# First sweep over the adjacency matrix in panels of 1024 rows with units of 256 columns, and a new assignment of its SBUF slots

## What is computed

```
d   = rsqrt(sum(adj, axis=1) + 1e-6)
L0  = (d[:,None] * (adj + I) * d[None,:]) @ (x @ w)
x1  = layernorm(x + L0)
agg = adj @ x1
msg = relu(agg @ W_msg.T + b_msg)
out = layernorm(x1 + gru_cell(msg, x1))
```

## Time and profile before

| | |
|---|---|
| median of 3 runs | 2015.1 us |
| the profiled execution | 2017.33 us, span 2015.3 us |
| granted TensorE clock, mean | 0.938 |
| PE busy | 1770.9 us (88%) |
| DVE busy | 1380.9 us (69%) |
| ACT busy | 640.4 us (32%) |
| HBM read | 545.79 MB, 273 GB/s over the span |

### The profile page before, as it was taken

How to read it: one execution, slowest core, us unless ns; L and a number is a source line. 1 busy time by engine, 2 the same in 40 slices (tenths; PEclk the granted TensorE clock), 3 DMA queues, 4 the chain that set the end, 5 groups by cost and what they waited for, 6 DMA issues and landing times.

```text
span 2015.3 us, 17025 instructions
## 1 busy us (share of the span) xinstructions
PE 1770.9 (88%) x6500; PEld 1200.8 (60%) x6500; DVE 1380.9 (69%) x1189; ACT 640.4 (32%) x561; POOL 130.5 (6%) x118
## 2 busy tenths in 40 slices
PE   0245777888888999999999999999999999999996
PEld 0123333434444444447888888888777777777774
DVE  6777776755576556558766666556678787878785
ACT  0000000000000000014444444444466565656563
POOL 0000000000000000012000000000000111011101
PEclk9767788888888999999999999999999999999998
DMA  9999999977789878755666666566799898989892
GB/s 356 387 373 353 339 341 335 335 250 251 255 311 320 298 260 300 273 190 189 199 194 200 200 201 195 189 197 192 260 358 311 289 323 296 316 287 326 294 318 78
DMA packets 284480, 551.12 MB, mean 273 GB/s; under 512 B 17648, under 2 KB 18160, under 8 KB 284400
## 3 DMA queue, kind: packets, MB, share of 16 engines
q1 hardware_dynamic: 280832, 541.13, 77.9%
q0 software_dynamic: 2560, 8.39, 1.2%
q10 hardware_dynamic: 1008, 0.53, 0.1%
HBM read 545.79 MB, written 4.19 MB: 273 GB/s over the span
## 4 chain that ended last, share of the span: by engine, by line
PE 76%; DMA 13%; SPq 6%; DVE 4%; issue 1%; ACT 1%; POOL 0%; DVEq 0%; ACTq 0%
PE bank L305 20%; PE bank L339 16%; PE bank L341 15%; PE bank L340 15%; DMA kept<-adj_blocks 8%; SPq L242 5%; DMA ring<-adj_blocks 3%; DVE colsum L591 3%; PE bank L292 2%; DMA spare<-adj_blocks 1%; DVE csum L595 1%; PE bank L404 1%; PE bank L417 1%; PE bank L415 1%; PE bank L410 1%
## 5 line engine op out<-in xcount | busy, mean ns | idle before, releaser
L601 DVE TENSOR_TENSOR lo<-ring,hi 128x2048 fp32r<-128x2048 f32 x204 | 465.4, 2288 | 265.4 <-ACT f L492 198.0
L486 ACT ACTIVATE hi<-ring 128x2048 fp32r<-128x2048 f32 x204 | 391.1, 1917 | 381.0 <-DMA ring<-adj_blocks 228.2
L339 PE MATMUL bank<-hi,x1s 128*128 128x512 f32 x1024 | 417.1, 407 | 6.1 <-DVE x1s L651 4.1
L341 PE MATMUL bank<-hi,x1s 128*128 128x512 f32 x1024 | 400.1, 391 | 0.0
L340 PE MATMUL bank<-lo,x1s 128*128 128x512 f32 x816 | 318.7, 391 | 0.0
L305 PE MATMUL bank<-kept,feat 128*128 128x512 f32 x608 | 294.9, 641 | 13.3 <-DMA kept<-adj_blocks 13.3
L591 DVE TENSOR_TENSOR colsum<-colsum,ring 128x2048 f32<-128x2048 f32 x106 | 243.0, 2293 | 77.8 <-DMA ring<-adj_blocks 77.8
L591 DVE TENSOR_TENSOR colsum<-colsum,kept 128x2048 f32<-128x2048 f32 x97 | 222.4, 2293 | 82.0 <-DMA kept<-adj_blocks 82.0
L305 PE MATMUL bank<-ring,feat 128*128 128x512 f32 x528 | 247.6, 625 | 18.6 <-DMA ring<-adj_blocks 18.6
L339 PEld LDWEIGHTS bank<-hi,x1s 128*128 128x128 f32 x1024 | 192.9, 188 | 56.2 <-issue 7.2
L465 ACT ACTIVATE dege<-bank 128x4 f32<-128x4 f32 x16 | 2.8, 174 | 685.1 <-PE bank L292 685.1
(11 more groups left out here) (87 smaller groups left out, 1394.7 us busy)
## 6 DMA issues: line engine op xcount, KB each, us to landing
ring<-adj_blocks SPq DMA_DIRECT2D x656, 512.0 KB, 6.1
kept<-adj_blocks SPq DMA_DIRECT2D x202, 512.0 KB, 8.4
more<-adj_blocks SPq DMA_DIRECT2D x104, 512.0 KB, 6.0
spare<-adj_blocks SPq DMA_DIRECT2D x62, 512.0 KB, 10.2
xt<-x_t SPq DMA_DIRECT2D x16, 256.0 KB, 8.1
xin<-x POOLq DMA_DIRECT2D x16, 256.0 KB, 3.5
out<-y POOLq DMA_DIRECT2D x16, 256.0 KB, 6.1
wih_s<-wih_t ACTq DMA_DIRECT2D x1, 192.0 KB, 6.5
```

Source lines behind the costliest of these rows:

```text
L339: pe.matmul(acc[:, :], fh, ah, start=start and c == 0, stop=False, skip_group_check=True)
L341: mm = pe.matmul(acc[:, :], fl, ah, start=False, stop=stop and c == KC - 1, skip_group_check=True)
L486: ins = act.activation(hi[:, n % NHI], raw(slot_of2[n]), ACT.Copy)
L601: ins = dve.tensor_tensor(flat(low(n)), flat(raw(slot_of2[n])), flat(hi[:, n % NHI]).bitcast(f32), ALU.subtract)
```

## The change

The first sweep goes by 8 panels of 1024 rows, each of 32 **units** of 256 columns: [128, 2, 1024], again 1 MB and the same work for DVE (one addition of 128x2048) and PE (2 column blocks x 2 halves of the rows, 4 matmuls of 128x512). A unit is one whole block of HBM, fetched by one DMA with runs of 8 KB. The number of panel ends goes from 16 to 8.

Early are all units left of the diagonal block, the 4 on it, and for panels 0 to 2 the 4 of the block right of it: 39 blocks of 1024 x 1024, or 156 tiles. N2 becomes 100. A burst has 8 units in panels 1 to 3 and 4 in the others.

There are 17 slots in panels 0 to 3 and 15 after; each unit gets the slot whose release the planner estimates to come first. The last 8 units take slots 4 to 11 only. The last three low units (LATE), not two, come behind the degrees. `xt` has one buffer of 1024 rows, and `load_xt(P+1)`, at the 17th unit of panel P, waits for `support(P)`, which PE runs behind the burst of panel P-1.

The second and third stages load as before, by tiles with runs of 2 KB; `split_hi` waits for the slots 12 to 14 that `hi` overlays.

```
-    def kept_tile(i, k):
-        return i <= k <= i + 2 and k - i <= depth(k)
-    RING1 = [0, 1, 2, 3, 10, 11, 12]
-    KEEP = [4, 5, 6, 7, 8, 9]
+    NP, NU, WP = N // 1024, 32, 1024
+    BAND = (0, 1, 2)
+    LATE = 3
+    def kept_unit(P, j):
+        return j // 4 == P or (P in BAND and j // 4 == P + 1)
+    def early_unit(P, j):
+        return j // 4 < P or kept_unit(P, j)
     def early(i, k):
-        return k < i or kept_tile(i, k)
+        return early_unit(i // 2, 2 * k)
     def panel_order(P):
+        low = list(range(4 * P))
+        far = [j for j in range(4 * P, NU) if not kept_unit(P, j)]
+        kept = [j for j in range(4 * P, NU) if kept_unit(P, j)]
+        head, tail = low[:max(0, 4 * P - LATE)], low[max(0, 4 * P - LATE):]
+        mixed = sorted([((q + 0.5) / len(head), 0, j) for q, j in enumerate(head)] +
+                       [((q + 0.5) / len(far), 1, j) for q, j in enumerate(far)])
+        body = [j for _, _, j in mixed]
+        cut = min(len(body), 20)
         return body[:cut] + kept + body[cut:] + tail
...
+    burst = {P: ([(P - 1, j) for j in range(4 * P, 4 * P + 4)] if P - 1 in BAND else []) +
+                [(P, j) for j in range(4 * P, 4 * P + 4)] for P in range(NP)}
...
+    come, pe_at = 0.0, 0.0
+    for P in range(NP):
+        for j in panel_order(P):
+            n = len(slot_of1)
+            slots = range(4, 12) if n >= NP * NU - 8 else range(17 if P < 4 else 15)
+            s = min(slots, key=lambda s: free[s])
...
+            come = max(come + 1, free[s] + 2.5)
+            if j < 4 * P:
+                pe_at = max(pe_at, come + (8 if j in after_degrees[P] else 0)) + 1.4
+                free[s] = pe_at
+            else:
+                free[s] = 1e9 if kept_unit(P, j) else come + 1
+        pe_at = max(pe_at, come + 6)
+        for t in burst[P]:
+            pe_at += 1.4
+            free[slot_of1[at1[t]]] = pe_at
...
             def load_xt(P):
-                if P >= 2:
-                    sp.wait_ge(supp_done, P - 1)
-                sp.dma_start(xt[:, P % 2, :], x_t[:, P * W:(P + 1) * W]).then_inc(xt_in[P % 2], 16)
+                if P:
+                    sp.wait_ge(supp_done, P)
+                sp.dma_start(xt[:, :], x_t[:, P * WP:(P + 1) * WP]).then_inc(xt_in, 16)
...
+            for n, (P, j) in enumerate(T1):
                 if before1[n] is not None:
                     slot_free1(before1[n])
                 s = slot_of1[n]
-                load(s, P, k)
+                sp.dma_start(unit(s), adj_blocks[P * NP + (P - j // 4) % NP, j % 4]).then_inc(slot_in[s], 16)
+                if n == 2:
                     load_xt(0)
+                if n % NU == 16 and P + 1 < NP:
                     load_xt(P + 1)
...
+            def product(P, j):
+                n = at1[(P, j)]
+                first = first_product[P] == (P, j) and P > 0
+                if first and P >= 2:
+                    pe.wait_ge(evicted, 2 * P - 2)
+                pe.wait_ge(slot_in[slot_of1[n]], loads1[n] * 16)
+                for u in range(2):
+                    for h in range(2):
+                        mm = pe.matmul(bank[P % 2 * 2 + h][:, :], feat0[:, j * 2 + u, :],
+                                       unit(slot_of1[n])[:, u, h * W:(h + 1) * W], start=first and u == 0,
+                                       stop=final_product[P] == (P, j) and u == 1, skip_group_check=True)
                 mm.then_inc(prod_done, 1)
...
+            for P in range(NP):
+                for j in before_degrees[P]:
+                    product(P, j)
                 degrees(P)
+                for j in after_degrees[P]:
+                    product(P, j)
+                pe.wait_ge(feat0_ready, P + 1)
+                for Q, j in burst[P]:
+                    if (Q, j) == (P, 4 * P):
+                        add_self(P)
+                    product(Q, j)
+                if P + 1 < NP:
                     support(P + 1)
...
             split_hi(0)
             split_hi(1)
+            evict(NP - 1)
             split_hi(2)
```

More of the change, by code:

```diff
@@ new lines, in gnn_resnorm_kernel @@
+    products = []
+    for P in range(NP):
+        products += [(P, j) for j in before_degrees[P] + after_degrees[P]] + burst[P]
+    product_no = {t: n + 1 for n, t in enumerate(products)}
+    first_product = {P: min((t for t in products if t[0] == P), key=lambda t: product_no[t]) for P in range(NP)}
+    final_product = {P: max((t for t in products if t[0] == P), key=lambda t: product_no[t]) for P in range(NP)}
+    free = {s: 0.0 for s in range(17)}
+    held, count = {}, {s: 0 for s in range(17)}
@@ L114, in gnn_resnorm_kernel @@
             first = (N2 % 4)
-            order = [(first + j) % 4 for j in range(4)] + [13, 14]
+            order = [(first + j) % 4 for j in range(4)] + [17, 18]
             s = order[(n - N2) % 6]
@@ L200, in raw, with unit @@
                 return kept[:, s - 4]
-            return spare[:, 0] if s == 12 else more[:, s - 13]
+            if s < 15:
+                return pool3[:, s - 12]
+            return spare[:, s - 15] if s < 17 else more[:, s - 17]
+        def raw(s):
+            return slot(s).rearrange("p (c r) -> p c r", c=KC)
+        def unit(s):
+            return slot(s).rearrange("p (u r) -> p u r", u=2)
         def low(n):
             s = slot_of2[n]
-            return lo[:, s] if s < 4 else more_lo[:, s - 13]
-        slot_in = [sem(f"slot_in{s}") for s in range(15)]
-        xt_in = [sem(f"xt_in{s}") for s in range(2)]
+            return lo[:, s] if s < 4 else more_lo[:, s - 17]
+        slot_in = [sem(f"slot_in{s}") for s in range(19)]
+        xt_in = sem("xt_in")
         xin_in = [sem(f"xin_in{s}") for s in range(2)]
@@ L289, in degrees @@
                     pe.wait_ge(deg_ready, P)
[L290 to L293, removed]
+                for b in range(WP // 128):
+                    mm = pe.matmul(p_deg[:, b:b + 1], csum[:, b * 128:(b + 1) * 128], ones[:, :], start=True, stop=True)
                 mm.then_inc(deg_done, 1)
[L296 to L307, removed]
-                mm.then_inc(prod_done, 1)
@@ L316, in add_self @@
             def add_self(P):
-                for c in range(KC):
-                    pe.matmul(bank[P % NACC][:, c * 128:(c + 1) * 128], feat0[:, P * KC + c, :], ident[:, :],
-                              start=P == 0 and c == 0, stop=False, skip_group_check=True)
+                for c in range(WP // 128):
+                    pe.matmul(bank[P % 2 * 2 + c // KC][:, c % KC * 128:(c % KC + 1) * 128],
+                              feat0[:, P * WP // 128 + c, :], ident[:, :],
+                              start=P == 0 and c % KC == 0, stop=False, skip_group_check=True)
@@ L754, in _ @@
             pool.wait_ge(zeroed, 4)
-            for P in range(NT):
+            for P in range(NP):
+                t0 = P * WP // 128
                 pool.wait_ge(deg_ready, P + 1)
-                pool.tensor_tensor(dinv[:, P * KC:(P + 1) * KC], dege[:, :], mhalf[:, :], ALU.pow)\
-                    .then_inc(dinv_ready, 1)
+                pool.tensor_tensor(dinv[:, t0:t0 + WP // 128], dege[:, :], mhalf[:, :], ALU.pow).then_inc(dinv_ready, 1)
             def load_rows(q):
```

176 lines of the change are left out of this document (72 added, 104 removed).

## The result

The changed kernel takes 1920.66 us (median of 4 runs, 1918.99 to 1921.81), the kernel before 2013.82 us (4 runs); the ratio is 0.9536, with a 95% interval of 0.9519 to 0.9552. The forecast was 1937 us, a gain of 80 us on the profiled span; that span went from 2015.3 to 1918.1 us, so the gain is 97.

A forecast was written before the change was run, and what follows sets the result against it. The prediction saw waits for slots and products leaving neither PE nor DMA full before 900 us. First sweep -98, seam +7.7, second stage +8.0, +1 and +1 gave -80 on 2017.3: 1937 us, range 1912 to 1988.

The forecast's parts named there:

- The price of a load: First-sweep loads: a 1 MB unit in 8 KB runs takes 2.55 us, ends 2.32 and 2.71.
- 105 units lie on the path (31 + 32 + 3 x 14): Panels 0 to 4: only these loads set the time, so 2.71 us each gives +17, 2.32 gives -24.
- PE's chain: Ends of panels 1 to 3: from the last unit's landing through degrees, low units and burst to `support`, 51.7 us.
- `load_xt` decides: Panels 2 to 4: SP's wait there for `support` sets the length, 95 us each where loads alone need 82.9.
- PE's panels: Panels 5 to 7, bound by PE: 87.6, 101.4 and 115.1 us from degrees to degrees.
- the 5 us that I added for low clock: Rest of the first sweep: PE's reduced clock adds 5 us, as in old panel 13; last product at 799.
- The seam: First sweep to second stage: T2[1] waits for a late slot; last product to `layer1(0)` 18.8 instead of 11.1 us, 7.7 lost.
- Given back in the second stage: Second stage: layer 0 of three more tiles costs 8.0 us, row 12 costs 1, a later GRU step 1.
- row 12: Second stage: its `x1` is needed at tile 7 but queued at tile 8 of DVE; 0 to 3 us, taken as 1.
- (a): Rival on first-sweep loads: 8 KB runs load no faster than 2 KB, 2.71 us a unit, 1954 us; chance 0.17.
- (b): Rival on slots: panels still wait for slots in turn, panels 5 and 6 take 120 us each, 1988 us; chance 0.15.
- (c): Rival on first-sweep loads: 8 KB runs lower the rate, 3.3 us a unit, slower than before at 2038 us; chance 0.06.

## Why the prediction came out as it did

**The price of a load.** Taken 2.55, measured 2.48 us. The term was mis-sized within its ends. Degrees of panel 4 came 11.2 us earlier than forecast. In panels 0 and 1 this is the price: together 3.7 us, for 63 loads x 0.07 = 4.4 (panel 0 alone is 1.3 late, as DVE starts late). Panels 2 to 4 were 7.4 us shorter in sum, where the 3 x 14 loads of my sum give 2.9; that all 160 loads x 0.07 make 11.2 is no proof, since another step was wrong there. Of the two figures in the Trainium skill (DMA: Bandwidth & Descriptors), the 425 GB/s of Bandwidth, Measured was nearly met (422). The same section says that about 358 GB/s is what each core gets when both cores of a pair stream. This program runs on one core, so the prediction was wrong to read the figure in Specifications as a bound for it.

**How many loads are on the path.** "105 units lie on the path (31 + 32 + 3 x 14)" is the step that failed. By it the 0.23 us between 2.71 and 2.48 are 24 us; the runs showed 46.6. I had let each of panels 2 to 4 start anew at the wait for `support`, with an empty queue and 5.9 us to the first unit. In the trace the queue isn't empty then; the hole lies 17 to 20 us long right behind a panel's end, where 15 of 17 slots are held, and the panel is 32 loads (79.4), 1.2 for `xt` and some 12 of hole and dip: 92. My sum of PE's chain was right (51.7 us to the end of `support`; measured from the last landing at 169.9 to 220.6, 50.7), but it isn't what the end of the panel hangs on; with 43 for what follows it gave 95 for another reason. I had both mechanisms in the text, and added up the wrong one. That 95 came near the measured 92 to 93 was luck; moving `load_xt` alone (-1.6 us) shows it.

**`load_xt` decides.** Wrong for this kernel, right for those with free slots: behind the first hole it is the next in line, at the same length. Two waits stood one behind the other, and either alone gives 91 to 93 us for panel 2.

**PE's panels.** Right to 0.3 us each, from one duration of 3.43 us per unit and 1.7 and 1.8 for the small steps. With the clock at 1.00 all through these panels, the 5 us that I added for low clock weren't there; they were taken from panel 13 before, where PE had idled.

**The seam.** Right to the tenth (18.8), and by its cause: the exchange of two slots took it away. The tenth is luck: with the same slots other executions show 18.9 to 21.8 us, as T2[1] lands sooner or later.

**Given back in the second stage.** +9.2 for 10 forecast. `layer1(7)` did not wait for row 12: no wait of PE for it stands in the trace.

**Rivals.** (a) is refuted as a fact (the rate did rise). Its time, 1954, was 13 us too early for the kernel with 2.71 us a load, by the count of loads above. (b) did not come true, because slots go by estimated release: with a fixed rotation the same panels are slower than the kernel before. The estimate has no `load_xt`, degrees or `support` in it and was good enough for panels 5 to 7. (c) did not occur.

So of the gain of 93 us 47 are the loads by one DMA with runs of 8 KB, measured with everything else in place. The other 46 are slots, panels and kept blocks together, net of the 8 us lost at the seam and the 9 behind it. How they part between fewer panel ends and more slots wasn't measured; with a fixed rotation the whole is a loss of 42.

## What to carry to other kernels

When two waits lie on one queue, the one that is longer in a table of waits need not be the one that costs: look for the stretch where the throughput of the resource falls, and name the wait that stands there. Change the price of a transfer in one run, and compare the response, panel by panel, with the number of transfers times the change: 15.3 us for 64 x 0.23 was the count itself, 11.4 us for 32 x 0.23 said that something else had grown with it. When another limit goes away, look at the granted clock of the engine that now waits: here that took back 3.3 us. In a planned assignment of buffers, look up what the first steps of the next stage inherit: one slot here cost 7.7 us, and an exchange of two numbers gave it back.

## What the runs showed of the hardware

Loads of 1 MB into 128 partitions from SP's queue, one core, run at 387, 409 and 422 GB/s with runs of 2, 4 and 8 KB (2.71, 2.56, 2.48 us per 1.05 MB), the first two in DMAs of 512 KB, the last in DMAs of 1 MB; whether 8 KB runs in smaller DMAs do as well wasn't tried. Beside such a stream the seven small loads of another queue at the start come later, the longer the runs: with 2, 4 and 8 KB the last was there at 12.2, 15.4 and 22.1 us. Idle time of PE shows in its clock: 68 matmuls took 18.96 us at granted clock 1.00 and 22.29 us at 0.85, the latter behind a wait of 3.0 us.
